# Low halves of the split activations: from two engines and two counters to VectorE and one counter

## The reference

```python
CONV_LAYERS = [(128, 10, 5), (128, 3, 2), (128, 3, 2), (128, 3, 2), (128, 3, 2), (128, 2, 2)]

def _block(x, cw, cb, gw, gb, stride):
    y = lax.conv_general_dilated(x, cw, (stride,), 'VALID', ...)
    y = y + cb[None, :, None]
    yg = y.reshape(B, NUM_GROUPS, C // NUM_GROUPS * T)
    mu = yg.mean(axis=-1, keepdims=True)
    var = yg.var(axis=-1, keepdims=True)
    yn = ((yg - mu) * lax.rsqrt(var + EPS)).reshape(B, C, T)
    yn = yn * gw[None, :, None] + gb[None, :, None]
    return jax.nn.gelu(yn)

h = x[:, None, :]
for (cw, cb, gw, gb), (_, _, s) in zip(conv_params, CONV_LAYERS):
    h = _block(h, cw, cb, gw, gb, s)
```

## Time and profile before

| | us |
|---|---|
| median of 3 runs | 1849.29 (1847.28 to 1850.98) |
| the profiled execution's own time | 1851.3 |
| its span, first to last instruction | 1849.7 |
| PE busy in the span | 1471.9 (80%) |
| VectorE (DVE) busy | 1063.5 (57%) |
| ScalarE (ACT) busy | 756.0 (41%) |
| GpSimd (POOL) busy | 605.8 (33%) |
| mean granted TensorE clock | 0.893 of full |

### The profile page before, as it was taken

The page is one execution under the profiler, slowest core; times in us unless marked ns, Lnnn a source line. Parts: engine busy times, 40 slices in busy tenths (PEclk is TensorE's granted clock), DMA queues, the critical chain, the costliest instruction groups (busy, mean ns, idle before and its releaser), DMA issues.

```text
span 1849.7 us, 32545 instructions
## 1 busy us (share of the span) xinstructions
PE 1471.9 (80%) x10013; PEld 1016.5 (55%) x10014; DVE 1063.5 (57%) x2234; ACT 756.0 (41%) x1456; POOL 605.8 (33%) x502
## 2 busy tenths in 40 slices
PE   5985599998774899989666999888649999249997
PEld 3332477783333677753334777733337778227775
DVE  5987445558894445569864545598844545202221
ACT  2653355525542555435533555265325553002321
POOL 3732133305431333236322333064223331421111
PEclk7997799998886999989877999899769999569999
DMA  4200121210000222110001221100014331721110
GB/s 120 92 1 1 34 59 42 58 36 12 1 1 1 61 58 50 35 38 1 1 1 34 62 62 45 38 1 1 1 28 109 94 90 53 222 59 45 49 50 17
DMA packets 105852, 81.31 MB, mean 44 GB/s; under 512 B 57842, under 2 KB 96267, under 8 KB 105747
## 3 DMA queue, kind: packets, MB, share of 16 engines
q1 hardware_dynamic: 99988, 70.65, 15.1%
q0 software_dynamic: 5760, 9.36, 1.7%
HBM read 34.66 MB, written 18.38 MB: 29 GB/s over the span
## 4 chain that ended last, share of the span: by engine, by line
issue 40%; PE 29%; POOL 17%; DMA 4%; SPq 3%; DVE 3%; ACT 2%; POOLq 0%; DVEq 0%; ACTq 0%
POOL arena L794 11%; PE ps L1679 5%; PE ps L1621 5%; PE ps L1833 4%; DMA arena<-arena 3%; PE ps L1653 3%; PE ps L1665 3%; PE ps L1813 2%; PE ps L1814 2%; POOL arena L778 2%; PE ps L1628 1%; POOL slot_scratch L848 1%; POOL arena L780 1%; SPq L600 1%; ACT arena L935 1%
## 5 line engine op out<-in xcount | busy, mean ns | idle before, releaser
L1726 PE MATMUL ps<-arena,cwt 128*128 128x504 f16 (+2 forms) x1776 | 403.3, 387 | 89.1 <-DVE arena L1181 59.5
L1726 PEld LDWEIGHTS ps<-arena,cwt 128*128 128x128 f16 x1776 | 177.4, 104 | 306.2 <-DVE arena L1181 66.1
L794 POOL TENSOR_TENSOR arena<-arena 128x1008 f16<-128x1008 f32 (+2 forms) x112 | 257.4, 2309 | 192.1 <-DVE arena L1181 192.1
L1206 DVE TENSOR_REDUCE nmax<-ps 128x1 f32<-128x128 f32 (+5 forms) x288 | 176.9, 614 | 195.4 <-PE ps L1656 195.4
L1679 PE MATMUL ps<-arena 128*128 128x64 f32 (+2 forms) x2016 | 259.8, 269 | 9.3 <-DVE arena L1214 5.1
L1679 PEld LDWEIGHTS ps<-arena 128*128 128x128 f32 (+2 forms) x2016 | 241.5, 188 | 26.1 <-issue 17.8
L1214 DVE COPY arena<-ps 128x512 f32<-128x512 f32 (+4 forms) x288 | 156.1, 542 | 85.8 <-PE ps L1665 81.4
L1184 DVE TENSOR_TENSOR arena<-arena 128x1008 f16<-128x1008 f32 (+2 forms) x88 | 200.3, 2277 | 3.0
L917 ACT ACTIVATE arena<-ps,nmax 128x128 f32<-128x128 f32 (+5 forms) x288 | 180.6, 627 | 44.3 <-DVE nmax L1206 43.4
L1653 PE MATMUL ps<-arena 128*128 128x512 f16 (+6 forms) x780 | 164.6, 314 | 42.4 <-DMA arena<-arena 21.5
L1181 DVE CAST arena<-arena 128x1008 f16<-128x1008 f32 (+4 forms) x200 | 175.6, 908 | 32.2 <-ACT arena L903 16.2
(11 more groups left out here) (250 smaller groups left out, 2120.3 us busy)
## 6 DMA issues: line engine op xcount, KB each, us to landing
arena<-arena SPq DMA_DIRECT2D x96, 187.5 KB, 3.0
arena<-arena SPq DMA_DIRECT2D x96, 93.8 KB, 2.6
slot_scratch<-empty_slot SPq DMA_DIRECT2D x1, 5775.0 KB, 18.6
arena<-in_L_ffn_w SPq DMA_DIRECT2D x8, 576.0 KB
arena<-in_L_ffn_w SPq DMA_DIRECT2D x8, 384.0 KB
arena<-slot_scratch SPq DMA_DIRECT2D x31, 96.5 KB, 1.9
arena<-slot_scratch SPq DMA_DIRECT2D x31, 96.0 KB, 2.0
xa<-in_x POOLq DMA_DIRECT2D x5, 468.8 KB, 4.3
```

Source lines behind the costliest of these rows:

```text
L794: g.tensor_tensor(low, src, high, ALU.subtract).then_inc(S["lo_pool"], 1)
L1206: v.reduce_max(nmax[0:m, k_:k_ + 1], slot(g)[0:m, 0:128 * i + m], AX.X, negate=True).then_inc(S["smax_done"], 1)
L1726: last = t.matmul(bank(g, k)[:, 0:c * PITCH].rearrange("p (r c) -> p r c", c=PITCH), cwt[layer][:, w, tap, :], parts[x][:, f:f + 2 * c - 1 ...
```

## The change

`low_engine`, `lows` and the counters `lo_dve` and `lo_pool` go. `split` on VectorE now casts and subtracts for every unit, and one counter `lo_done` counts all low halves; as VectorE makes them in the order of `SPLITS`, its value for a unit is that unit's place. GpSimd's `low_parts` is gone from all layers. The three places that waited on the two old counters (ScalarE before it refills a stage buffer, VectorE before `halo`, PE before the low terms) wait on the new one. So 112 subtractions, 28 in each batch, leave GpSimd's queue and enter VectorE's, each right behind its cast. The arithmetic is the same.

```diff
-def low_engine(layer, piece):
-    if layer == 0:
-        return DVE_ENGINE if piece % 3 == 2 else "pool"
-    return "pool" if piece % 2 else DVE_ENGINE
...
     "hi_done": (0, len(SPLITS), 0, 0, 0),
-    "lo_dve": (0, sum(low_engine(*u) == DVE_ENGINE for u in SPLITS), 0, 0, 0),
-    "lo_pool": (0, sum(low_engine(*u) == "pool" for u in SPLITS), 0, 0, 0),
+    "lo_done": (0, len(SPLITS), 0, 0, 0),
...
-                def low_parts(layer):
-
-                    for unit in SPLITS:
-                        if unit[0] == layer and low_engine(*unit) == "pool":
-                            wait(pool, "hi_done", TOWER, SPLITS.index(unit) + 1, b)
-                            src, high, low = split_views(*unit)
-                            g.tensor_tensor(low, src, high, ALU.subtract).then_inc(S["lo_pool"], 1)
-
-
...
                 load_samples((b + 1) & (BATCH - 1))
-                low_parts(0)
                 for n in range(1, CONV_LAYERS):
                     group_rstd(TOWER, n, b)
-                    low_parts(n)
...
                             wait(act, "hi_done", TOWER, SPLITS.index(had_it) + 1, b)
-                            if low_engine(*had_it) == DVE_ENGINE:
-                                wait(act, "lo_dve", TOWER, lows(DVE_ENGINE, had_it), b)
-                            else:
-                                wait(act, "lo_pool", TOWER, lows("pool", had_it), b)
+                            wait(act, "lo_done", TOWER, SPLITS.index(had_it) + 1, b)
...
                 v.tensor_copy(high, src).then_inc(S["hi_done"], 1)
-                if low_engine(*unit) == DVE_ENGINE:
-                    dve.wait_ge(S["hi_done"], at("hi_done", TOWER, n, b))
-                    v.tensor_tensor(low, src, high, ALU.subtract).then_inc(S["lo_dve"], 1)
+                dve.wait_ge(S["hi_done"], at("hi_done", TOWER, n, b))
+                v.tensor_tensor(low, src, high, ALU.subtract).then_inc(S["lo_done"], 1)
 
             def wait_split(unit, b):
                 wait(dve, "hi_done", TOWER, SPLITS.index(unit) + 1, b)
-                for engine, name in ((DVE_ENGINE, "lo_dve"), ("pool", "lo_pool")):
-                    if lows(engine, unit):
-                        wait(dve, name, TOWER, lows(engine, unit), b)
+                wait(dve, "lo_done", TOWER, SPLITS.index(unit) + 1, b)
...
                                 if (tap, w, x) == (0, 0, 1):
-                                    for engine, name in ((DVE_ENGINE, "lo_dve"), ("pool", "lo_pool")):
-                                        wait(pe, name, TOWER, lows(engine, unit), b)
+                                    wait(pe, "lo_done", TOWER, SPLITS.index(unit) + 1, b)
```

More of the change, by code:

```diff
@@ L231 @@
 }
-def lows(engine, unit):
-    return sum(low_engine(*u) == engine for u in SPLITS[:SPLITS.index(unit) + 1])
 def split_unit_of(layer, row):
```

## The result

| | before | after |
|---|---|---|
| median | 1848.28 (1847.01 to 1850.98, 4 runs) | 1817.47 (1816.05 to 1818.75, 4 runs) |
| profiled execution's own time | 1851.3 | 1816.93 |
| its span | 1849.7 | 1815.3 |
| mean granted TensorE clock | 0.893 | 0.892 |

The ratio, the changed kernel's time over that of the kernel before, is 0.9831 (95% interval 0.9814 to 0.9848): faster by 30.8 us between the medians and by 34.4 us between the two profiled executions. The forecast was 1810, in a range of 1802 to 1820.

The account below looks back on a forecast made before the run. VectorE was taken to set the first stage's pace, its subtractions standing behind GpSimd's. Savings of 25 (first stage), 11.5 (layer 2) and 2.7 (layer 3) make 39 us: 1812 from the profiled 1851.3, 1810 as median, range 1802 to 1820.

Parts of the forecast that it names:

- Rival 2: VectorE's subtraction: the long time is its own and stays 2.28 us, so the kernel gets slower, 2000 us; chance 0.04.
- The unit: VectorE's cast with its wait, 0.67 us, plus a subtraction of 1.13 us: 1.80 us for 1008 columns.
- First stage: Layers 0 and 1: the later of VectorE's and PE's bounds sets the end; 25 us saved over four batches.
- S: The start of the first cast in the first stage, from which the forecast counts that stage's bounds in us.
- PE in batches 1 to 3, where the clock is up by then: S + 58.4: First stage: PE's matmuls would end at S + 58.4, below VectorE's bound of S + 59.4.
- Rival 1: First stage: PE becomes the bound and small delays on both engines lose 13 us, giving 1823 us; chance 0.15.
- Layer 3: Seven units on VectorE go from about 12.5 to 11.1 us; 0.9 us saved in each of three batches, 2.7 us.
- But PE is next: its idle time ahead of the last nine matmuls is 0.40: Layer 3: PE limits the gain to between 0.4 and 1.4 us a batch; 0.9 taken.
- In batch 3 nothing is won: Layer 3: PE runs 63 matmuls in one piece of 14.59 us in that batch, so no time is saved.
- Layers 4 and 5: The odd units' subtractions join VectorE's queue, but PE's pace sets layer 4's end; 0 saved in both layers.
- Rival 3: First stage: TensorE's clock falls to its lower level for a change in its gaps, about 2015 us; chance 0.02.
- Rival 4: Layers 3 to 5: the clock rises earlier, or the interplay costs nothing, 8 us more saved, 1802 us; chance 0.06.

Follow-up runs that it names:

- the other execution: The changed kernel run once more without any edit, also called the second execution; measured 1818.40 us, ratio 0.9836.
- the kernel with light statistics: The changed kernel with convolution 1's statistics reading one row of each four, 125 columns in place of 500; measured 1817.24 us, ratio 0.9831.
- the fills: The changed kernel with useless matmuls of 504 columns around the small group-norm matmul of each layer; measured 1807.34 us, ratio 0.9782.
- 1817.97: The changed kernel with five useless matmuls of 504 columns ahead of the first job of convolution 1; measured 1817.97 us, ratio 0.9836.

## Why the prediction was right where it was, and where not

**The mechanism: right.** The forecast read a subtraction of 1.21 us with GpSimd at rest and one of 2.86 that ended 1.07 us behind GpSimd's, and took the difference for standing. After the change the subtraction of 1008 columns takes 1208 ns at the median and 1211 at most. Useless work on GpSimd brings the standing back, 208 us of it. Rival 2 falls.

**The unit: 1.84 us, not 1.80.** The cast with its wait is 0.71, not 0.67; I had taken half of a pair of casts, which overlap by a little, where a lone cast is 0.68 long with 0.03 behind it. So every term that counts units of VectorE's queue came out too small: layer 1's units took 22.3 us where 21.9 stood, and layer 2 gave 9.6, not 11.5.

**First stage: 22.1 for 25.** VectorE's queue sets the end, as forecast for batches 1 to 3, and its bound becomes 24 x 1.84 + 16 x 0.585 + 0.2 + 6.6 = S + 60.3, not S + 59.4; measured is S + 60.34 to 60.35. Three times 0.9 us is 2.8 of the 2.9 that are missing: the mis-sized unit. For batch 0 the forecast had PE's bound, S + 60.8; measured is S + 60.5, and S + 60.35 in the other execution. A second step failed and cost nothing by itself: "PE in batches 1 to 3, where the clock is up by then: S + 58.4". With the low halves made early PE has nothing to do between convolution 0 and the third cast (2.36 us in batch 1), the granted clock falls from 0.96 to 0.50, and the first job takes 1.7 us more, S + 60.1; the kernel with light statistics, where PE does end the stage, has S + 60.09. That is 0.25 us below VectorE's bound, not 1.0, which is why no edit of one engine alone took more than that off the time from S to the end. Rival 1 said that PE becomes the bound, by small delays on both sides at 0.8 us a pair of blocks. The bounds did come within 0.25 us of each other, but without such a loss: two blocks take 14.51, which is 6 x 1.84 + 6 x 0.585, to 0.04.

**Layer 3: 5.1 for 2.7, in part luck.** VectorE's seven units went from 12.5 to 11.3, as forecast but for the unit's size. The step that failed is "But PE is next: its idle time ahead of the last nine matmuls is 0.40". The 0.40 us was a wait, and I took it for the cover that PE leaves; but PE's 54 matmuls ahead of it, 11.96 us long in batch 0 of before, themselves stood behind low halves. With these made early, and the clock up in time (1.00 in the window 144 to 146 of batch 0), the last nine start 0.13 to 0.24 us behind the halo copies in all four batches of the first execution, and 1.2 to 1.3 us was won four times. How much was won went with the moment of the clock's rise. "In batch 3 nothing is won" rested on one piece of 14.59 us, a batch in which the clock rose late (0.50 from 1309 to 1315 us); in the first execution after the change it rose in time there (0.50 from 1277 to 1280.5, 1.00 from 1281 on), and 1.3 us was won. In batch 0 of the second execution it rose late (0.77 in the window 146 to 148), the piece was 14.49 us, and nothing was won. So the forecast's idea that PE can be next was right, its size (0.9 three times) was not worked out from when the clock rises, and the second execution's 3.4 us lies nearer to it.

**Layers 4 and 5: -0.5 for 0.** PE ends layer 4 as forecast: its last nine matmuls start 0.3 to 0.6 us behind the halo copies. The -0.4 is smaller than the 0.9 us by which this layer varies.

**The rest: -1.9 for 0.** The setup ahead of the first batch was 1.4 us longer. Over the profiled executions of the kernels without extra work on GpSimd it lies between 35.9 and 38.0, so that is not the change's. The attention part was longer by 0.2 a batch.

**The sum.** 22.1 + 9.6 + 5.1 - 0.5 - 1.9 is 34.4, for 39: the two terms mis-sized by VectorE's unit cost 4.8 us, layer 3 gave 2.4 back, the rest took 2.4. That layer 3 and the rest cancel is chance. A further 2.5 us of the 7.5 between 1810 and 1817.47 lies in the step from the profiled execution to the median. I took before's as 2 us above its median; it was 3.0 above, and the changed kernel's is 0.5 below. Rival 3 (the clock falls in the whole stage) didn't come: the window 66 to 82 has 1.00. It fell at one place, at the stage's beginning. Rival 4 would have needed the fills: with them PE's clock is higher (a mean of 0.931 for 0.892), and in layers 3 and 4 VectorE takes most of the gain (PE waits 0.50 and 1.08 us for the halo copies).

## What to carry to other kernels

When two engines take turns at one kind of work, lay their timelines side by side and look for an instruction that ends a fixed time after the other engine's (here 1.07 us). Take its length where the other is at rest, here 1.21 us and not the mean of 2.28. Help that makes the helped engine stand is worth its work less that standing, here 127 less 154 us. Then work out every stage's bound for both engines with the new lengths, once with the clock as it stands and once with it fallen behind a gap that grows (here to 0.50, with one of 2.36 us): where two bounds lie as close as here, 0.25 us apart in 60, the next edit on either engine alone gives next to nothing, as 1817.24 and 1817.97 showed. And a wait in the trace isn't slack: ask what the work ahead of it had waited for.

## What was not expected of the hardware

- The standing moves. With GpSimd under way first VectorE's subtraction stands (2.92 us); with VectorE's 0.05 us ahead, GpSimd's does (3.34 for 2.34), and then the next cast (2.80 for 0.68).
- A GpSimd memset of 1008 fp16 columns, 0.93 us, holds up a VectorE cast (1.54 for 0.68), and a one-column operation on GpSimd takes 1.22 us behind a subtraction.
- After a wait of 2.36 us the granted clock fell from 0.96 to 0.50, in a stage that is busy from there on. With five matmuls in the wait the job behind it took 4.00 us for 5.69. In the kernel before, with waits of 1.71 and 1.57 us there, the clock stayed at 1.00; in batch 2 of the kernel with layer 0 as before it fell to 0.50 with waits of 1.36 and 1.58 us. So what decides it isn't shown.
- Two executions of one kernel differ in when the clock rises in a layer: PE's 63 matmuls of layer 3 took 13.27 us in one and 14.49 in the other, with VectorE's work the same.
- A mean granted clock of 0.931 for 0.892 went with 10 us of 1817. In layers 3 and 4 VectorE limits what it brings, as PE's waits of 0.50 and 1.08 us for the halo copies show; about half of the gain lies in the attention part, where its cause isn't shown.
